# Two attention layers on 64 graphs: both plain fp32 products split in three passes, with a new order of the first slot, the steady slot and the drain

## The chip, the cores and the metric

One NeuronCore of a Trainium2 chip runs the whole program. The metric is the device time of one execution in microseconds; the kernel before takes 312.04 us (median of 3 runs, 311.88 to 312.27). Names of engines: PE is TensorE, DVE is VectorE, ACT is ScalarE, POOL is GpSimd, SP is SyncE, which here issues every DMA.

## The reference, cut to what matters

```python
def reference(x, adj, nodemask, Wqk, Wv, Wq_w, Wq_b, Wk_w, Wk_b, Wv_w, Wv_b):   # x (64,128,256), adj (64,128,128)
    # layer 0
    q, k = split(x @ Wqk); v = x @ Wv
    agg = einsum('bij,bjd->bid', adj, k * mask)
    w = mask * einsum('bid,bid->bi', q, agg) / 16
    x = layernorm(x + softmax(w, axis=1)[:, :, None] * v)
    # layer 1
    query, key, value = x @ Wq_w.T + Wq_b, x @ Wk_w.T + Wk_b, x @ Wv_w.T + Wv_b
    weight = adj * exp(einsum('bqd,bkd->bqk', query, key))
    weight = weight / sum(weight, axis=2)
    return layernorm(x + einsum('bqk,bkd->bqd', weight, value))
```

## The kernel before

The 64 graphs are taken in 32 pairs. The program on each engine is a list of slots, t = -2 to 29, and then a `drain()` written out by hand. A slot works on several pairs at once: layer 0 of pair t+2, the normalisation between the layers of pair t+1, queries, values and scores of pair t, the attention product of pair t-1, and the output of pair t-3. Slots 4 to 27 are a hardware loop unrolled four times; the others stand written out, and slots with r of -2, -1, 0 and DRAIN (29) have steps of their own. There is no scheduler: the order on each engine is the order of the code in `slot(t, r)`, and semaphores bind the engines.

Weights are folded first: layer 0's scores need only `x·(Wq Wk^T)·(adj x)`, so `aggregate` forms adj·x, `project` forms x·M0 and x·Wv together (512 columns), and `weight` on DVE multiplies and sums. `transpose_w`, a row maximum, `exp_row` on ACT, `inv_sum` and `p_row` on DVE make the softmax over the nodes, `transpose_p` turns it into a column, and `sum_x1` adds p·v to x. Statistics (`both_stats`, `neg_mean`, `var_eps`) are on DVE, the root and the shift (`rstd`, `shift`) on POOL, and the normalisation itself (`norm`) on ACT.

Most products are already split: an operand is written as hi + lo in the format F32R, and `split_half` (L748 to L750) runs hi·hi, hi·lo and lo·hi. Two products of each slot are plain fp32 matmuls: `aggregate` (L765) and `attend` (L845). One plain fp32 product shows in the trace as two matmul records, so the two graphs of a pair make four. On PE the slot is: transposes of x1, aggregate, project graph 0, attend, project graph 1, queries, transpose_w, values, scores, transpose_p. The two halves of a split are made by copies to F32R on ACT or DVE (`x1t_hi` L537, `xt_hi` L390) and by a subtraction on DVE or POOL (`x1t_lo` L539, `xt_lo` L344). POOL's slot holds five instructions: `rstd`, `shift`, `xt_lo`, `x1b` (x1 plus the value bias) and `adjm` (adj times the mask).

Of the kernel before, what the change touches and what calls it, by code (L numbers as in the profile page):

```python
# [32 lines left out]
def build(nc, x_pairs, xt_pairs, adjt_pairs, params0, params1, value_bias, out_pairs):  # L33
    ctx = ExitStack()
    with ctx:  # L35
# [348 lines left out]
        def _(act):  # L384
            def split_xt(u, r):

                act.wait_ge(xt_loaded[r % 2], transfers2(u, r))
# [4 lines left out]

# [23 lines left out]
            def drain():  # L416
# [12 lines left out]
                act.wait_ge(x1t_lo_done, b + 1)
                nc.scalar.copy(x1t[:, :, :, :], x1t_drain_ps).then_inc(x1t_copied, 1)  # L430
                act.wait_ge(val_done, a + 1)
                nc.scalar.copy(val[:, :, 0:DIM], val_ps[:, :, 0:DIM]).then_inc(val_copied, 1)
                act.wait_ge(z_done, b + 1)
                bias_z(z_b)
# [565 lines left out]
```

## Time and profile before

| | |
|---|---|
| median of 3 runs | 312.04 us |
| the profiled execution | 311.97 us |
| its span, first to last instruction | 310.1 us |
| busy: PE | 298.0 us (96%) |
| busy: DVE, ACT, POOL | 223.6 (72%), 195.8 (63%), 143.2 (46%) |
| granted TensorE clock, mean | 0.993 |

The span is the time between the first and the last instruction; the profiled execution takes 1.87 us more than that. A busy share is a mean over the whole span. Durations of single instructions overlap their neighbours on the same engine by some hundredths to tenths of a microsecond, so what an instruction costs its engine is the distance from its start to the next start, where nothing is waited for.

### The profile page before, as it was taken

To read this page: it belongs to the slowest core of one execution; us is meant where nothing else is said; L and a number is where in the kernel's file an instruction comes from. 1 tells how busy PE (TensorE), PEld (TensorE's weight loads), DVE (VectorE), ACT (ScalarE), POOL (GpSimd) and SP (SyncE) were. 2 spreads that over 40 slices of the span, in tenths; PEclk is the share of its full clock that TensorE was granted. 3 is DMA by queue.
4 is the path that set the end of the run, shared out by engine and by line. 5 is a ranking of instruction groups with operands and counts; after the bars stand their busy time and mean duration, and the time that the engine had idled before them with its cause. 6 is when DMAs were issued, how large, how long until landed. Compare 5 with 4: busy or idle time off the path is not lost. (4 is left out here: it accounts for less than half of the span.)

```text
span 310.1 us, 6526 instructions
## 1 busy us (share of the span) xinstructions
PE 298.0 (96%) x1900; PEld 269.3 (87%) x1900; DVE 223.6 (72%) x691; ACT 195.8 (63%) x453; POOL 143.2 (46%) x181
## 2 busy tenths in 40 slices
PE   8997999999999999999999999999999999999891
PEld 6876999999998999999998999999999999999780
DVE  2475778777778877777788777778877777788565
ACT  4354556676666666766666676666666766665761
POOL 2365554345555444455543345555443455542522
PEclk9999999999999999999999999999999999999997
DMA  6921224232434332234333222444423234210012
GB/s 231 327 71 35 85 88 116 52 113 83 118 119 119 119 91 80 80 105 119 119 119 111 83 73 90 118 119 119 119 85 83 81 107 119 85 53 36 34 36 101
DMA packets 19165, 31.26 MB, mean 101 GB/s; under 512 B 2128, under 2 KB 6608, under 8 KB 19152
## 3 DMA queue, kind: packets, MB, share of 16 engines
q1 hardware_dynamic: 19152, 31.11, 32.8%
q8 instruction: 6, 0.10, 0.1%
q14 instruction: 7, 0.06, 0.1%
HBM read 22.71 MB, written 8.39 MB: 100 GB/s over the span
## 5 line engine op out<-in xcount | busy, mean ns | idle before, releaser
L336 POOL TENSOR_TENSOR rstd<-var_eps,minus_half 128x4 f32<-128x4 f32 x31 | 31.5, 1018 | 138.6 <-DVE var_eps L669 124.5
L396 ACT ACTIVATE x<-x_sum,shift,rstd 128x256 f32<-128x256 f32 x62 | 34.0, 595 | 52.2 <-POOL shift L339 52.2
L748 PE MATMUL ps<-w_hi,xt_hi 128*128 128x512 f32 x128 | 61.6, 481 | 0.5 <-DVE w_lo L734 0.5
L750 PE MATMUL ps<-w_hi,xt_lo 128*128 128x512 f32 x128 | 50.4, 394 | 0.0
L749 PE MATMUL ps<-w_lo,xt_hi 128*128 128x512 f32 x128 | 50.2, 393 | 0.0
L275 POOL TENSOR_TENSOR x1b<-x,bv_all 128x512 f32<-128x512 f32 x32 | 41.5, 1297 | 4.3 <-DVE x L568 3.1
L344 POOL TENSOR_TENSOR xt_lo<-xt_raw,xt_hi 128x512 fp32r<-128x512 f32 x31 | 40.0, 1291 | 3.3 <-ACT xt_hi L390 3.3
L748 PE MATMUL ps<-wv_hi,x1t_hi 128*128 128x258 f32 x124 | 37.8, 304 | 0.0
L396 ACT ACTIVATE x<-x,shift,rstd 128x256 f32<-128x256 f32 x62 | 33.8, 595 | 3.5 <-POOL shift L287 3.5
L750 PE MATMUL ps<-wv_hi,x1t_lo 128*128 128x258 f32 x124 | 35.3, 285 | 0.0
L748 PE MATMUL ps<-x1t_hi,at_hi 128*128 128x256 f32 x124 | 35.1, 283 | 0.0
L749 PE MATMUL ps<-wv_lo,x1t_hi 128*128 128x258 f32 x124 | 35.1, 283 | 0.0
L749 PE MATMUL ps<-x1t_lo,at_hi 128*128 128x256 f32 x124 | 35.0, 282 | 0.0
L750 PE MATMUL ps<-x1t_hi,at_lo 128*128 128x256 f32 x124 | 34.8, 281 | 0.0
L409 ACT ACTIVATE z<-ps,z_bias 128x256 f32<-128x256 f32 x62 | 26.0, 470 | 11.3 <-PE ps L750 11.3
L524 DVE CUSTOM_DVE_ANT_0 agg<-ps,agg,adjt 128x256 f32<-128x256 f32 x64 | 30.9, 484 | 2.9 <-PE ps L750 0.8
L765 PE MATMUL ps<-x_raw,adjm 128*128 128x256 f32 x128 | 32.9, 380 | 0.0
L840 PE MATMUL ps<-x1t,z 128*128 128x128 f32 x240 | 31.8, 275 | 0.6 <-ACT z L409 0.6
L845 PE MATMUL ps<-val,edge 128*128 128x258 f32 x124 | 32.1, 380 | 0.0
L549 DVE SCALAR_TENSOR_TENSOR x_sum<-ps,p_col,x_raw 128x256 f32<-128x256 f32 x64 | 28.0, 479 | 3.2
L840 PEld LDWEIGHTS ps<-x1t,z 128*128 128x128 f32 x240 | 29.3, 191 | 0.8 <-ACT z L409 0.8
L748 PEld LDWEIGHTS ps<-w_hi,xt_hi 128*128 128x128 f32 x128 | 24.1, 188 | 5.7 <-issue 0.9
(121 smaller groups left out, 668.8 us busy)
## 6 DMA issues: line engine op xcount, KB each, us to landing
xt_raw<-xt_pairs SPq DMA_DIRECT2D x32, 256.0 KB, 2.7
x_raw<-x_pairs SPq DMA_DIRECT2D x32, 256.0 KB, 2.7
out_pairs<-x SPq DMA_DIRECT2D x31, 256.0 KB, 2.1
adjt<-adjt_pairs SPq DMA_DIRECT2D x32, 129.0 KB, 2.1
p<-params SPq DMA_DIRECT2D x1, 770.0 KB, 6.8
p<-params SPq DMA_DIRECT2D x1, 512.0 KB, 3.9
p<-params SPq DMA_DIRECT2D x1, 256.0 KB, 4.9
out_pairs<-x SPq DMA_DIRECT2D x2, 128.0 KB, 1.8
```

The lines of the kernel that those rows point to most:

```text
L275: nc.gpsimd.tensor_tensor(x1b[r % 2][:, :].rearrange("p (g d) -> p g d", g=2), x1[r % 2][:, :].rearrange("p (g d) -> p g d", g=2), bv_all[ ...
L336: nc.gpsimd.tensor_tensor(rstd[r % 2][:, :, :], var_eps[:, :, :], minus_half[:, :, :], ALU.pow)\
L344: nc.gpsimd.tensor_tensor(xt_lo[(r + 3) % 2][:, :, :, :].rearrange("p t g n -> p (t g n)"), xt_raw[(r + 3) % 2][:, :], xt_hi[(r + 3) % 2][ ...
L396: last = nc.scalar.activation(out[:, graph(g)], in_[:, graph(g)], ACT.Identity, bias=shift[r % 2][:, layer, g:g + 1], scale=rstd[r % 2][:, ...
L524: nc.vector.tensor_tensor_reduce(agg[:, g, :], y_ps(r)[:, g, :], agg[:, g, :], adjt[r % 4][:, PAIR_N + g:PAIR_N + g + 1], 0.0, ALU.mult, A ...
L549: nc.vector.scalar_tensor_tensor(out=x1_sum[r % 2][:, graph(g)], in0=v0_ps(r)[:, g, :], scalar=p_col[:, g:g + 1], in1=x_raw[r % 4][:, grap ...
L748: nc.tensor.matmul(out, s_hi, m_hi, start=first, stop=False)
L749: nc.tensor.matmul(out, s_hi, m_lo, start=False, stop=False)
L750: return nc.tensor.matmul(out, s_lo, m_hi, start=False, stop=last)
L765: mm = nc.tensor.matmul(agg_ps[:, g, :], adjm[r % 2][:, graph(g, NODES)], x_raw[r % 4][:, graph(g)], start=True, stop=True)
L840: mm = nc.tensor.matmul(out[:, g, :], zs[:, k, graph(g, NODES)], xs[:, k, g, :], start=(k == 0), stop=(k == HALVES - 1))
L845: return nc.tensor.matmul(out[:, g, 0:VAL_COLS], edges[:, graph(g, NODES)], vals[:, g, :], start=True, stop=True)
```

## The change

Six things change.

1. `aggregate` for pairs 4 to 31 (`SPLIT = 4`) and `attend` for pairs 0 to 28 become split products of three passes. The last three pairs keep the plain attend.
2. The halves that these need are new instructions. ACT: `edge_hi` (128x256), `adjm_hi` (128x256), `x_hi` (128x512). POOL: `low_x` makes `x_lo` (128x512), then `edge_lo` and, in `low_adjm`, `adjm_lo` (128x256 each). DVE: `val_lo` (128x512, from PSUM).
3. On PE the attention product stands behind both projections instead of between them, and the transposes of the next pair's x1 stand at the end of a slot instead of the head of the next one.
4. `exp_row` moves from SBUF to PSUM; both `weight` instructions stand together ahead of `attended`; POOL's `adjm` stands ahead of `xt_lo`.
5. First slot: `fold_biases` comes later, `transpose_w` of pair 2 stands behind the values, `bias_z` stands ahead of the norm, and POOL waits for `x1t_lo` before its first `x1b`.
6. Drain: the roles of the two last pairs' buffers are exchanged, and the attention product of pair 30 and what DVE does with it stand before the values of pair 31 and its edges.

```diff
@@ pool @@
             def slot(t, r):
+                if exists(t + 3) and r + 3 >= SPLIT:
+                    low_x(t + 3, r + 3)
+                if exists(t - 1):
+                    pool.wait_ge(edge_hi_done, t)
+                    nc.gpsimd.tensor_tensor(edge_lo[:, :], edge[:, :], edge_hi[:, :].bitcast(F32), ALU.subtract)\
+                        .then_inc(edge_lo_done, 1)
...
+                if r == -1:
+                    mask_adj(3, 3)
+                    pool.wait_ge(x1t_lo_done, 1)
...
-                if exists(t + 3) and r >= 0:
-                    mask_adj(t + 3, r + 3)
+                if exists(t + 3) and r + 3 >= SPLIT:
+                    low_adjm(t + 3, r + 3)
@@ act @@
+                if exists(t - 1):
+
+                    act.wait_ge(edge_done, t)
+                    if exists(t - 2):
+                        act.wait_ge(sum_done, t - 1)
+                    nc.scalar.copy(edge_hi[:, :], edge[:, :]).then_inc(edge_hi_done, 1)
...
+                if exists(t + 3) and r + 3 >= SPLIT:
+                    split_adjm(t + 3, r + 3)
...
+                if exists(t + 4) and r + 4 >= SPLIT:
+                    split_x(t + 4, r + 4)
@@ dve @@
+                if exists(t - 1):
+
+                    dve.wait_ge(val_copied, t)
+                    nc.vector.tensor_tensor(val_lo[:, :, 0:DIM], val_ps[:, :, 0:DIM], val_hi[:, :, 0:DIM].bitcast(F32),
+                                            ALU.subtract).then_inc(val_lo_done, 1)
...
-                    nc.vector.tensor_scalar(p_row[0:2, :], exp_row[:, :], inv_sum[:, 0:1], None, ALU.mult)\
+                    nc.vector.tensor_scalar(p_row[0:2, :], exp_row_ps(r + 2), inv_sum[:, 0:1], None, ALU.mult)\
                         .then_inc(p_row_done, 1)
@@ pe @@
+                        mm = split_product(agg_ps[:, g, :], [(adjm_hi[r % 2][:, n], adjm_lo[r % 2][:, n],
+                                                              x_hi[r % 2][:, graph(g)], x_lo[r % 2][:, graph(g)])])
...
                 if exists(t + 2):
                     project(t + 2, r + 2, 1)
+                if exists(t - 1):
+
+                    pe.wait_ge(edge_lo_done, t)
+                    pe.wait_ge(val_lo_done, t)
+                    for g in range(2):
+                        n = graph(g, NODES)
+                        mm = split_product(sum_ps[:, g, 0:VAL_COLS], [(edge_hi[:, n], edge_lo[:, n],
+                                                                       val_hi[:, g, :], val_lo[:, g, :])])
+                    mm.then_inc(sum_done, 1)
@@ drain, pe @@
                 pe.wait_ge(x1t_lo_done, b + 1)
-                pe.wait_ge(z_copied, a + 1)
                 queries(x1t_hi, x1t_lo)
-                pe.wait_ge(x2_done, DRAIN + 1)
-                scores(score_ps, z, x1t_a)
+                pe.wait_ge(edge_done, a + 1)
                 pe.wait_ge(val_copied, a + 1)
+                attend(sum_a_ps, edge_a, val_a, 0)
+                attend(sum_a_ps, edge_a, val_a, 1).then_inc(sum_done, 1)
                 pe.wait_ge(score_bias_done, a + 1)
                 values(x1t_hi, x1t_lo, 0)
```

POOL's slot in the loop before, from the copy of one slot's `xt_lo` on (a trailing number is the buffer):

```order
L344 TENSOR_TENSOR xt_lo0<-xt_raw0,xt_hi0 128x512
L275 TENSOR_TENSOR x1b0<-x1_0,bv_all 128x512
...
L267 TENSOR_TENSOR adjm0<-adjt0 128x256
...
L336 TENSOR_TENSOR rstd0<-var_eps,minus_half 128x4
L339 TENSOR_TENSOR shift0<-neg_mean,rstd0 128x4
```

The same stretch on POOL after the change:

```order
L374 TENSOR_TENSOR xt_lo1<-xt_raw1,xt_hi1 128x512
L287 TENSOR_TENSOR x1b1<-x1_1,bv_all 128x512
L342 TENSOR_TENSOR adjm_lo1<-adjm1,adjm_hi1 128x256
...
L347 TENSOR_TENSOR x_lo0<-x_raw0,x_hi0 128x512
L355 TENSOR_TENSOR edge_lo<-edge,edge_hi 128x256
...
L364 TENSOR_TENSOR rstd1<-var_eps,minus_half 128x4
L367 TENSOR_TENSOR shift1<-neg_mean,rstd1 128x4
...
L279 TENSOR_TENSOR adjm0<-adjt0 128x256
```

Between the last big instruction of one slot and `rstd` of the next there was nothing; now `x_lo` follows straight behind `adjm_lo`, and `edge_lo` behind it.

DVE in the loop before, from the column p of pair t+1 to the variance:

```order
L544 COPY p_col<-ps 128x2
L549 SCALAR_TENSOR_TENSOR x1_sum0<-ps,p_col,x_raw0 128x256 x2
L651 TENSOR_TENSOR edge<-exp_s,adjt2 128x256
L537 CAST x1t_hi<-x1t 128x512
L539 TENSOR_TENSOR x1t_lo<-x1t,x1t_hi 128x512
L530 BN_STATS stats<-x1_sum0 128x6
L668 TENSOR_SCALAR neg_mean<-stats 128x4
L669 TENSOR_SCALAR var_eps<-stats 128x4
```

and the same stretch after:

```order
L604 COPY p_col<-ps 128x2
L609 SCALAR_TENSOR_TENSOR x1_sum0<-ps,p_col,x_raw0 128x256 x2
L713 TENSOR_TENSOR edge<-exp_s,adjt2 128x256
L597 CAST x1t_hi<-x1t 128x512
L599 TENSOR_TENSOR x1t_lo<-x1t,x1t_hi 128x512
L720 TENSOR_TENSOR val_lo<-ps,val_hi 128x2x256
L590 BN_STATS stats<-x1_sum0 128x6
L735 TENSOR_SCALAR neg_mean<-stats 128x4
L736 TENSOR_SCALAR var_eps<-stats 128x4
```

`val_lo` is new and stands ahead of the statistics; the others keep their places.

## Rows read from the trace of the kernel before

**Rows 1.** Windows: stretch, length, busy us PE PEld DVE ACT POOL, clock, DMA, GB/s

```profile
47.69:280.42 232.73, 232.73 (x1511) 212.46 (x1510) 176.06 (x547) 157.04 (x364) 111.64 (x130) 1.00 0.34 100
```

**Rows 2.** Timeline of PE, one slot (start us, us, what)

```profile
155.63 1.03 PE L765 MATMUL ps<-x_raw,adjm 128*128 128x256 f32 x4
...
156.73 0.39 PE L749 MATMUL ps<-w_lo,xt_hi 128*128 128x512 f32 x1
...
157.88 1.03 PE L845 MATMUL ps<-val,edge 128*128 128x258 f32 x4
...
160.15 0.29 PE L748 MATMUL ps<-x1t_hi,at_hi 128*128 128x256 f32 x1
...
161.58 0.27 PE L791 MATMUL ps<-ident,w_col 128*2 128x128 f32 x1
```

**Rows 3.** Timeline of DVE, same slot

```profile
156.46 0.41 DVE L651 TENSOR_TENSOR edge<-exp_s,adjt 128x256 f32<-128x256 f32 x1
156.79 0.42 DVE L537 CAST x1t_hi<-x1t 128x512 fp32r<-128x512 f32 x1
157.24 0.69 DVE L539 TENSOR_TENSOR x1t_lo<-x1t,x1t_hi 128x512 fp32r<-128x512 f32 x1
157.85 0.70 DVE L530 BATCH_NORM_STATS2 stats<-x_sum 128x6 f32<-128x512 f32 x1
158.58 0.17 DVE L668 TENSOR_SCALAR neg_mean<-stats 128x4 f32<-128x4 f32 x1
```

**Rows 4.** Timeline of POOL, same slot

```profile
158.91 1.02 POOL L336 TENSOR_TENSOR rstd<-var_eps,minus_half 128x4 f32<-128x4 f32 x1 [4.48 <-DVE var_eps L669]
160.00 0.20 POOL L339 TENSOR_TENSOR shift<-neg_mean,rstd 128x4 f32<-128x4 f32 x1
160.15 1.29 POOL L344 TENSOR_TENSOR xt_lo<-xt_raw,xt_hi 128x512 fp32r<-128x512 f32 x1
161.41 1.31 POOL L275 TENSOR_TENSOR x1b<-x,bv_all 128x512 f32<-128x512 f32 x1
162.65 0.63 POOL L267 TENSOR_TENSOR adjm<-adjt 128x256 f32<-128x256 f32 x1
```

**Rows 5.** Timeline of ACT, same slot

```profile
160.23 1.10 ACT L396 ACTIVATE x<-x_sum,shift,rstd 128x256 f32<-128x256 f32 x2 [1.44 <-POOL shift L339]
161.78 0.84 ACT L409 ACTIVATE z<-ps,z_bias 128x256 f32<-128x256 f32 x2 [0.45 <-PE ps L750]
```

**Rows 6.** Timelines of POOL and of DVE, where the two meet

```profile
7.08 1.17 DVE L734 TENSOR_TENSOR w_lo<-p,w_hi 128x256 fp32r<-128x256 f32 x2
...
7.14 0.83 POOL L267 TENSOR_TENSOR adjm<-adjt 128x256 f32<-128x256 f32 x1 [5.50 <-DMA adjt<-adjt_pairs]
...
20.73 1.31 POOL L275 TENSOR_TENSOR x1b<-x,bv_all 128x512 f32<-128x512 f32 x1
...
20.90 1.43 DVE L537 CAST x1t_hi<-x1t 128x512 fp32r<-128x512 f32 x1
```

**Rows 7.** Timelines of PE and POOL, slots 0 and 1

```profile
26.07 0.27 PE L791 MATMUL ps<-ident,w_col 128*2 128x128 f32 x1 [1.29 <-DVE w_col L524]
...
28.41 1.16 PE L840 MATMUL ps<-x1t,z 128*128 128x128 f32 x8 [0.62 <-ACT z L409]
...
33.61 1.02 POOL L336 TENSOR_TENSOR rstd<-var_eps,minus_half 128x4 f32<-128x4 f32 x1 [4.06 <-DVE var_eps L669]
```

**Rows 8.** Timelines of POOL, PE and DVE, slot 29 and drain

```profile
284.23 1.02 POOL L336 TENSOR_TENSOR rstd<-var_eps,minus_half 128x4 f32<-128x4 f32 x1 [4.57 <-DVE var_eps L669]
...
288.91 0.30 PE L797 MATMUL ps<-ident,p_row 128*128 128x128 f32 x1
...
289.73 0.22 DVE L717 TENSOR_SCALAR score_bias<-ps,s_bias 128x2 f32<-128x2 f32 x1 [0.96 <-ACT val L503]
...
301.60 0.42 DVE L555 TENSOR_TENSOR edge_b<-exp_s,adjt 128x256 f32<-128x256 f32 x1 [0.74 <-ACT exp_s L403]
...
304.03 0.16 DVE L563 RECIPROCAL den_inv<-ps 128x2 f32<-128x2 f32 x1
```

More of the change, by code:

```diff
@@ L73, in build @@
         adjm = [sb(f"adjm{i}", [128, PAIR_N]) for i in range(2)]
+        x_hi = [sb(f"x_hi{i}", [128, PAIR_X], F32R) for i in range(2)]
+        x_lo = [sb(f"x_lo{i}", [128, PAIR_X], F32R) for i in range(2)]
+        adjm_hi = [sb(f"adjm_hi{i}", [128, PAIR_N], F32R) for i in range(2)]
+        adjm_lo = [sb(f"adjm_lo{i}", [128, PAIR_N], F32R) for i in range(2)]
         agg = sb("agg", [128, 2, DIM])
@@ L92, in build @@
         edge = sb("edge", [128, PAIR_N])
+        edge_hi = sb("edge_hi", [128, PAIR_N], F32R)
+        edge_lo = sb("edge_lo", [128, PAIR_N], F32R)
+        val_hi = sb("val_hi", [128, 2, VAL_COLS], F32R)
+        val_lo = sb("val_lo", [128, 2, VAL_COLS], F32R)
         den_inv = sb("den_inv", [128, 2])
@@ L326, in drain, with low_adjm, low_x @@
                 root(DRAIN, 0)
-            def slot(t, r):
+            def low_adjm(u, r):
+                pool.wait_ge(adjm_hi_done, u + 1 - SPLIT)
+                nc.gpsimd.tensor_tensor(adjm_lo[r % 2][:, :], adjm[r % 2][:, :],
+                                        adjm_hi[r % 2][:, :].bitcast(F32), ALU.subtract).then_inc(adjm_lo_done, 1)
+            def low_x(u, r):
+                pool.wait_ge(x_hi_done, u + 1 - SPLIT)
+                nc.gpsimd.tensor_tensor(x_lo[r % 2][:, :], x_raw[r % 4][:, :],
+                                        x_hi[r % 2][:, :].bitcast(F32), ALU.subtract).then_inc(x_lo_done, 1)
+            def slot(t, r):
+                if exists(t + 3) and r + 3 >= SPLIT:
[4 more added lines that the diff above has]
+                        .then_inc(edge_lo_done, 1)
                 if exists(t + 1) or exists(t - 2):
@@ L391, in split_xt, with split_x, split_adjm @@
                                xt_raw[r % 2][:, :]).then_inc(xt_hi_done, 1)
+            def split_x(u, r):
+                act.wait_ge(x_loaded[r % 4], transfers4(u, r))
+                act.wait_ge(agg_done, u - 1)
+                nc.scalar.copy(x_hi[r % 2][:, :], x_raw[r % 4][:, :]).then_inc(x_hi_done, 1)
+            def split_adjm(u, r):
+                act.wait_ge(adjm_done, u + 1)
+                act.wait_ge(agg_done, u - 1)
+                nc.scalar.copy(adjm_hi[r % 2][:, :], adjm[r % 2][:, :]).then_inc(adjm_hi_done, 1)
             def norm(out, in_, layer, r, done):
@@ L425, in drain @@
                 act.wait_ge(z_done, a + 1)
-                bias_z(z)
+                bias_z(z_a)
+                act.wait_ge(val_done, a + 1)
+                nc.scalar.copy(val_a[:, :, 0:DIM], val_ps[:, :, 0:DIM]).then_inc(val_copied, 1)
                 normed_out(DRAIN - 1, n + 1)
[L429 to L434, printed above, removed]
                 act.wait_ge(score_done, a + 1)
@@ L489, in slot @@
                     act.wait_ge(row_max_done, t + 3)
-                    nc.scalar.activation(exp_row[:, :], w_row_ps(r + 2), ACT.Exp, bias=neg_max[:, 0:1],
+                    nc.scalar.activation(exp_row_ps(r + 2), w_row_ps(r + 2), ACT.Exp, bias=neg_max[:, 0:1],
                                          accum_out=exp_sum[:, 0:1]).then_inc(row_exp_done, 1)
+                if exists(t + 3) and r + 3 >= SPLIT:
+                    split_adjm(t + 3, r + 3)
                 if r == DRAIN:
@@ L615, in drain @@
                 variance(1)
-                weigh_edges(a, edge)
-                bias_scores(b)
-                weigh_edges(b, edge_b)
                 dve.wait_ge(sum_done, a + 1)
-                attended(a, sum_ps)
+                attended(a, sum_a_ps)
                 dve.wait_ge(x2_done, a + 1)
@@ L957, in _ @@
             fold_scores(1).then_inc(at_done, 1)
-            fold_biases()
+            aggregate(1, 1)
             transpose_p(0, 0)
-            aggregate(1, 1)
             project(1, 1, 0)
             project(1, 1, 1)
+            fold_biases()
+            transpose_w(1, 1)
             aggregate(2, 2)
-            transpose_w(1, 1)
+            transpose_next(-1, -1)
             slots(pe, slot, 0)
```

142 lines of the change are left out of this document (83 added, 59 removed).

## The prediction

> **What bounds the kernel now.** I read the clock first: the granted TensorE clock is 1.00 in the steady stretch [rows 1], the level of 2.4 GHz, so the clock is not the matter. Then the busy time by stretch. From 47.69 to 280.42 us, 26 slots by the transposes of p, PE is busy for 232.73 of 232.73 us [rows 1]; that is 8.951 us a slot, and PE sets it. DVE has 176.06, ACT 157.04 and POOL 111.64 us of work in it, 6.77, 6.04 and 4.29 us a slot. Last I read the timelines of one slot: on POOL `rstd` waited 4.48 us for the variance [rows 4], ACT's norm 1.44 us for the shift and `z` 0.45 us for PE [rows 5]. The others run after PE with slack. A slot can also be counted from `rstd` to `rstd`: 33.61 in slot 1 [rows 7] and 284.23 in slot 29 [rows 8], 250.62 us for 28 slots, 8.951 again. I count in these below. The question is whether PE still sets the slot once DVE, ACT and POOL carry the work of making the halves.
>
> **The change, part by part.**
>
> PE's saving. The aggregate takes from 155.63 to 156.73, less one 512-column pass (156.73 to 157.88 is five passes of 0.23), so 0.87. The attend takes from 157.88 to 160.15, less six passes of 0.23, so 0.89. Split, each becomes six passes of 256 or 258 columns; twelve such passes take 160.15 to 161.58, 0.119 each [rows 2], so 0.72. The saving is 0.15 + 0.17 = 0.32 a slot: if PE stays the bound, a slot takes 8.63.
>
> ACT's additions. `edge_hi` and `adjm_hi` are 256 columns, `x_hi` is 512. I bound them by `z`, two instructions of 256 columns in 0.84 us: 4 x 0.42 = 1.68 us a slot at most, and by the slope alone, without what an instruction costs at its start, some 1.0. ACT had waits of 1.44 and 0.45 in the slot [rows 5]. I take 1.2 and put it off the path, since the shift comes later anyway (next part); uncovered it would be worth some tenths a slot.
>
> POOL's additions. `x_lo` is as large as `xt_lo`, 1.29 us; `edge_lo` and `adjm_lo` are as large as `adjm`, 0.63 [rows 4]. That is 2.55 us on 4.29, 6.8 of 8.9. By the sum it fits. By its place it may not. From `rstd` on POOL now runs without a gap: `rstd` 1.09 (158.91 to 160.00), `shift` 0.15, `adjm` 0.58 (0.63 less 0.05, the overlap with the next), `xt_lo` 1.26 (160.15 to 161.41), `x1b` 1.24 (to 162.65), `adjm_lo` 0.58, and then `x_lo` for 1.29. The sum is 6.19 us after the start of `rstd` [rows 4]. Before, POOL was idle in that last part, and there DVE makes `edge`, `x1t_hi` and `x1t_lo` [rows 3].
>
> POOL and DVE in one another's way. Two places of the trace show what happens when they meet [rows 6]. A cast of 512 columns SBUF to SBUF, 0.42 us in the slot [rows 3], took 1.43 from 20.90, under POOL's `x1b` of 20.73 to 22.04; it ended at 22.33, 0.29 after POOL. The second of two subtractions with both operands in SBUF ended at 8.25, 0.28 after POOL's `adjm` (7.97), and `adjm` itself took 0.83 instead of 0.63, from behind the first of them [rows 6]. So such an instruction on DVE does not end before POOL's current one has, and vice versa. `edge` and `x1t_lo` have two operands in SBUF and `x1t_hi` is that cast. `val_lo` reads PSUM for one operand; I take it as free of this.
>
> The Trainium skill, SBUF — State Buffer, section "Who interferes with whom", says that a DVE instruction with two SBUF inputs or in a two-port mode and a GpSimd instruction exclude each other, and that the loser waits for the other's whole length. The rows agree on who is blocked, but the blocked one ended 0.28 us after the other where a full one takes 0.41; by the page's words each block would cost 0.13 more and the sum below would be 27 x 0.13 = 3.5 us higher.
>
> Now the path. On ACT `exp_s` stands behind `x_hi`, and `edge` needs `exp_s`; POOL's `x_lo` needs only `x_hi`. So `edge` always comes when `x_lo` has begun or POOL is still in front of it. Then the loop from one `rstd` to the next is: 6.19 to the end of `x_lo`; 0.28 to the end of `edge`; `x1t_hi` begins 0.08 before that (156.46 + 0.41 against 156.79) and takes 0.45 to the next start, `x1t_lo` 0.61, `val_lo` 0.61 (as `x1t_lo`), the statistics 0.73, and `neg_mean` and the variance 0.33 to the start of `rstd` (158.58 to 158.91) [rows 3, 4]. Sum: 6.19 + 0.28 - 0.08 + 0.45 + 0.61 + 0.61 + 0.73 + 0.33 = 9.12 us. That is longer than PE's 8.63 and also than the 8.951 of before. I take 9.15, since `x_lo` also waits for `x_hi`, which comes about when POOL is free. `val_lo` is the one term without a row of its own: its bounds are 0.33 (as `edge` to the next start, for 256 columns) and 0.73 (the statistics of 512), so 8.84 to 9.24.
>
> Slots. `x_lo` is made in slots 1 to 28, so 27 distances from slot 1 to slot 28 take 9.15 and the last one PE's 8.65: 255.7 us against 250.62, **+5.1**.
>
> Start. In slot 0 PE waited 1.29 us for the weights and 0.62 for `z` [rows 7]; `transpose_w` now stands behind the values and `bias_z` ahead of the norm, and both waits should go, -1.91. In slot 1 `val_lo` (0.61) and the first block of `edge` (0.33, an estimate: 9.12 less the 8.79 that the loop has without it, rival a) are already in the way: **-0.97** in all.
>
> Drain. PE is no longer late in slot 29, so `z` follows the norm without its wait of 0.45 [rows 5]: -0.45. `p_col` stood behind `score_bias`, which waited 0.96 us for the copy of the values, until 289.73 + 0.13, where the transpose of p (288.91) had ended by 289.2 [rows 8]; now `p_col` is ahead: -0.6. The attend of pair 30 comes before the values of pair 31 and costs PE 0.89 there, but the values of pair 30 need not be finished between, and scores and queries only change places; I count 0. At the end `edge_b` was ready at 302.02; with an attend of 0.88 and 0.2 of latency the sum could be read at 303.1, but DVE took it up at 304.03, busy with pair 30 [rows 8]. Pair 30 is now done earlier: -0.8 (bounds 0 and -0.9). Drain: **-1.85**.
>
> Other edits. `exp_row` in PSUM, the order of `weight`, `neg_max` and `stats2`, and `adjm` ahead of `xt_lo` I cost at nothing: DVE has 2.2 us free a slot, less 0.6 for `val_lo`. The transposes of x1 at a slot's end instead of its head are the same work in the same place. The attend behind both projections is free as long as PE has slack; `edge_lo` and `val_lo` must be there about 3.5 us after the aggregate begins.
>
> **The sum.** The profiled execution took 311.97 us, 1.87 more than its span of 310.1, and stands 0.07 below the median of 312.04. 311.97 - 0.97 + 5.1 - 1.85 = 314.25: I forecast 314.2 us. A measurement of this kernel can tell about 0.2% (0.6 us) from no change.
>
> **Rivals.**
>
> (a) `edge` slips in ahead of `x_lo`, and only the cast is held. Then the loop is 6.19 + 0.29 + 0.03 + 0.61 + 0.61 + 0.73 + 0.33 = 8.79. For it: POOL may come late to `x_lo`, since `x_hi` is the last in ACT's slot. Against: `exp_s` is behind `x_hi`. Slots 27 x 8.79 + 8.65 = 246.0, -4.6; start -1.3, drain -1.85: 304.2 us.
>
> (b) PE stays the bound; nothing of POOL is on the path. 28 x 0.32 = -9.0, start -1.9, drain -1.4 (the wait of `z` stays): 299.7 us. For it: by busy time nothing else is full. Against: the loop above has 0.5 us too much.
>
> (c) `edge_lo` gets in between `x1t_hi` and `x1t_lo`. `edge_hi` takes about 0.37 from the end of `edge`, and with 0.08 for the two hand-overs `edge_lo` is ready 0.45 after it; `x1t_lo` begins 0.37 after it. If POOL wins, `x1t_lo` ends at 0.45 + 0.63 + 0.56 instead of 1.06 and every slot is 0.58 longer: 27 x 0.58 = +15.7, 329.9 us. This decides at 0.08 us. The same page of the Trainium skill says that issue order decides who blocks; by that `x1t_lo` wins, and the time stays at the forecast.
>
> (d) The gains at both ends don't come, because other waits stand behind those removed: +2.8, 317.0 us.
>
> **Chances.** Forecast 0.52, with its own range 311 to 318 (the bounds of `val_lo` and of the block); (a) 0.20, (b) 0.11, (c) 0.10, (d) 0.07. Of the forecast's 0.52 I put 0.38 above 312.7, 0.08 within 0.6 us of 312.04, and 0.06 below. Slower: 0.38 + 0.10 + 0.07 = 0.55; same 0.08; faster 0.06 + 0.20 + 0.11 = 0.37. The range is 303.5 to 321: it takes in (a) and (d) and leaves out (b) and (c).
>
> **What the new profile would show.** PE idle some 0.5 us a slot, most of it ahead of the aggregate, for `adjm_lo` of POOL; `edge` at 1 us or more instead of 0.41, ending 0.28 after `x_lo`; `rstd` to `rstd` 9.15; the matmul records of aggregate and attend at 0.12 spacing; `x1t_lo` at its 0.69. I would be wrong if `edge` still takes 0.41 (rival a or b), if PE is busy throughout (b), or if `x1t_lo` takes more than 1 us (c). At the ends: no wait of PE above 0.5 us in slot 0, and the last `den_inv` within 1.2 us of the end of the last edges.

## The result, and the profile after

The changed kernel takes 316.99 us (median of 4 runs, 316.78 to 317.20), the kernel before 311.96 in the same comparison (4 runs, 311.78 to 312.27). The ratio is 1.016 with a 95% interval of 1.0143 to 1.0178: 1.6% slower, 5.0 us, where I had forecast 2.2. The profiled execution took 316.78 us, with a span of 315.0 against 310.1.

The page of the kernel after, busy time by engine (us, share of the span, instructions):

```profile
PE 300.7 (95%) x2014; PEld 269.4 (86%) x2014; DVE 252.1 (80%) x720; ACT 218.3 (69%) x538; POOL 228.5 (73%) x269
```

The stretch that answers to [rows 1], 26 slots from `rstd` to `rstd`, in the same columns:

```profile
41.03:281.81 240.78, 236.56 (x1614) 212.65 (x1614) 203.77 (x573) 177.81 (x442) 190.21 (x208) 1.00 0.31 97
```

The granted clock is again 1.00, so it is not the matter. PE now sits idle for 4.22 us, which it did not before. POOL went from 4.29 to 7.3 us of work a slot (190.21 / 26), and with 1.9 us left no sum of busy times names it as the bound.

The span splits at `rstd` of slot 1 and of slot 29, as in the prediction:

| part | before | after | difference | forecast |
|---|---|---|---|---|
| start, to `rstd` of slot 1 | 33.61 | 31.84 | -1.77 | -0.97 |
| slots 1 to 29 | 250.62 | 258.60 | +7.98 | +5.1 |
| `rstd` of slot 29 to the end | 25.87 | 24.56 | -1.31 | -1.85 |
| span | 310.1 | 315.0 | +4.9 | +2.3 |

Timeline of POOL after, one slot, what answers to [rows 4] (start us, us, engine, line, what, the idle time before it and its releaser):

```profile
142.97 1.02 POOL L364 TENSOR_TENSOR rstd<-var_eps,minus_half 128x4 f32<-128x4 f32 x1 [1.06 <-DVE var_eps L736]
144.07 0.20 POOL L367 TENSOR_TENSOR shift<-neg_mean,rstd 128x4 f32<-128x4 f32 x1
144.22 0.61 POOL L279 TENSOR_TENSOR adjm<-adjt 128x256 f32<-128x256 f32 x1
144.79 1.29 POOL L374 TENSOR_TENSOR xt_lo<-xt_raw,xt_hi 128x512 fp32r<-128x512 f32 x1
146.04 1.27 POOL L287 TENSOR_TENSOR x1b<-x,bv_all 128x512 f32<-128x512 f32 x1
147.27 0.73 POOL L342 TENSOR_TENSOR adjm_lo<-adjm,adjm_hi 128x256 fp32r<-128x256 f32 x1
147.96 1.28 POOL L347 TENSOR_TENSOR x_lo<-x_raw,x_hi 128x512 fp32r<-128x512 f32 x1
150.04 1.15 POOL L355 TENSOR_TENSOR edge_lo<-edge,edge_hi 128x256 fp32r<-128x256 f32 x1 [0.80 <-ACT edge_hi L517]
152.25 1.02 POOL L364 TENSOR_TENSOR rstd<-var_eps,minus_half 128x4 f32<-128x4 f32 x1 [1.05 <-DVE var_eps L736]
```

Timeline of DVE after, same slot, what answers to [rows 3]:

```profile
148.55 0.98 DVE L713 TENSOR_TENSOR edge<-exp_s,adjt 128x256 f32<-128x256 f32 x1
149.45 0.41 DVE L597 CAST x1t_hi<-x1t 128x512 fp32r<-128x512 f32 x1
149.90 0.69 DVE L599 TENSOR_TENSOR x1t_lo<-x1t,x1t_hi 128x512 fp32r<-128x512 f32 x1
150.50 0.69 DVE L720 TENSOR_TENSOR val_lo<-ps,val_hi 128x512 fp32r<-128x512 f32 x1
151.10 0.71 DVE L590 BATCH_NORM_STATS2 stats<-x_sum 128x6 f32<-128x512 f32 x1
151.85 0.17 DVE L735 TENSOR_SCALAR neg_mean<-stats 128x4 f32<-128x4 f32 x1
```

Read the two together. From `rstd` at 142.97 POOL has no gap until `x_lo` ends at 149.24. `edge`, 0.41 us long before, was begun under `x_lo` and ended at 149.53, 0.29 after it. From there DVE has no gap to the variance, and that releases the next `rstd`. This closed loop of two engines, each of which is idle at some other point of the slot, takes 9.28 us here.

The same tiles over the whole program (duration in ns: shortest, median, longest):

```profile
L713 DVE TENSOR_TENSOR edge<-exp_s,adjt x29: 415/981/1007, 28.7 to 287.4; 128x256 f32<-128x256 f32 x29
L355 POOL TENSOR_TENSOR edge_lo<-edge,edge_hi x29: 737/1143/1150, 29.7 to 288.9; 128x256 fp32r<-128x256 f32 x29
L342 POOL TENSOR_TENSOR adjm_lo<-adjm,adjm_hi x28: 716/738/753, 36.1 to 286.1; 128x256 fp32r<-128x256 f32 x28
```

`edge` is held in 28 of its 29 cases; only the last, at 0.415, is not. `edge_lo` is held too, by `x1t_lo` ahead of it, but POOL has 1.05 us to spare there. (In e4 below, where `x1t_lo` reads PSUM, `edge_lo` takes 0.74.)

PE in the same slot, the transposes of x and the first passes of the aggregate, which answer to the head of [rows 2]:

```profile
147.31 0.63 PE L898 MATMUL ps<-ident,x 128*128 128x128 f32 x4
148.06 0.38 PE L813 MATMUL ps<-x_hi,adjm_hi 128*128 128x256 f32 x1
148.28 0.28 PE L814 MATMUL ps<-x_lo,adjm_hi 128*128 128x256 f32 x1
148.40 0.28 PE L815 MATMUL ps<-x_hi,adjm_lo 128*128 128x256 f32 x1
```

The waits of PE in the stretch (us in total, times, longest us):

```profile
PEld ps L813 <- POOL adjm_lo L342: 7.6, 20, 0.4
```

The aggregate waits for `adjm_lo`, which ends at 148.00. The busy figure shows little of it: the record of the transposes runs to 147.94, and only the 0.12 us behind that counts as idle.

### The profile page after: what moved, and what is told of

It is laid out like the page before. It is cut to its first block and busy times, and to the rows that moved or that the text cites. A ratio compares the mean times of both kernels' runs of the same rounds, so it can differ in the third digit from the quotient of the medians.

```text
span 315.0 us, 7064 instructions
## 1 busy us (share of the span) xinstructions
PE 300.7 (95%) x2014; PEld 269.4 (86%) x2014; DVE 252.1 (80%) x720; ACT 218.3 (69%) x538; POOL 228.5 (73%) x269
## 5 line engine op out<-in xcount | busy, mean ns | idle before, releaser
L813 PE MATMUL ps<-w_hi,xt_hi 128*128 128x512 f32 x128 | 50.7, 396 | 0.7 <-DVE w_lo L799 0.7
L355 POOL TENSOR_TENSOR edge_lo<-edge,edge_hi 128x256 fp32r<-128x256 f32 x29 | 32.0, 1102 | 25.3 <-ACT edge_hi L517 25.3
L347 POOL TENSOR_TENSOR x_lo<-x_raw,x_hi 128x512 fp32r<-128x512 f32 x28 | 36.2, 1292 | 0.1
L916 PE MATMUL ps<-x1t,z 128*128 128x128 f32 x248 | 35.6, 286 | 0.0
L916 PEld LDWEIGHTS ps<-x1t,z 128*128 128x128 f32 x248 | 30.0, 191 | 4.2 <-ACT z L456 2.4
L584 DVE CUSTOM_DVE_ANT_0 agg<-ps,agg,adjt 128x256 f32<-128x256 f32 x64 | 28.6, 482 | 1.0 <-PE ps L815 1.0
L815 PEld LDWEIGHTS ps<-w_hi,xt_lo 128*128 128x128 f32 x128 | 24.0, 188 | 5.3
```

The costliest lines, as they stand in the source:

```text
L347: nc.gpsimd.tensor_tensor(x_lo[r % 2][:, :], x_raw[r % 4][:, :], x_hi[r % 2][:, :].bitcast(F32), ALU.subtract).then_inc(x_lo_done, 1)
L355: nc.gpsimd.tensor_tensor(edge_lo[:, :], edge[:, :], edge_hi[:, :].bitcast(F32), ALU.subtract)\
L584: nc.vector.tensor_tensor_reduce(agg[:, g, :], y_ps(r)[:, g, :], agg[:, g, :], adjt[r % 4][:, PAIR_N + g:PAIR_N + g + 1], 0.0, ALU.mult, A ...
L813: nc.tensor.matmul(out, s_hi, m_hi, start=first, stop=False)
L815: return nc.tensor.matmul(out, s_lo, m_hi, start=False, stop=last)
L916: mm = nc.tensor.matmul(out[:, g, :], zs[:, k, graph(g, NODES)], xs[:, k, g, :], start=(k == 0), stop=(k == HALVES - 1))
```

## The experiments

The slot is (`rstd` of slot 29 less `rstd` of slot 1) / 28, from the profile of each. Each ratio is to the runs of before in the same comparison, whose medians lie between 311.96 and 312.25 us.

| kernel | us (range) | ratio to before, 95% | slot, us | `edge`, median us |
|---|---|---|---|---|
| before | 311.96 (311.78 to 312.27) | 1 | 8.951 | 0.415 |
| after | 316.99 (316.78 to 317.20) | 1.016 (1.0143 to 1.0178) | 9.236 | 0.981 |
| e1_neither | 307.11 (306.65 to 307.57) | 0.9828 (0.9812 to 0.9845) | 8.887 | 0.416 |
| e2_attend_only | 304.01 (303.86 to 304.14) | 0.9734 (0.9717 to 0.9750) | 8.780 | 0.415 |
| e3_aggregate_only | 304.80 (304.78 to 305.08) | 0.9762 (0.9746 to 0.9779) | 8.796 | 0.703 |
| e4_psum_both | 310.97 (310.82 to 311.38) | 0.9959 (0.9944 to 0.9973) | 9.011 | 0.415 |
| e5_xlo_behind | 319.00 (318.92 to 319.21) | 1.0220 (1.0203 to 1.0237) | 9.301 | 0.415 |
| e6_psum_edge | 308.35 (308.20 to 308.46) | 0.9876 (0.9859 to 0.9892) | 8.931 | 0.415 |
| e7_early_adjm | 316.01 (315.99 to 316.60) | 1.0123 (1.0106 to 1.0140) | 9.211 | 0.54 |
| e8_two_pool_extras | 307.21 (306.93 to 307.39) | 0.9840 (0.9823 to 0.9856) | 8.883 | 0.614 |
| e9_adjm_lo_ahead | 317.67 (317.50 to 317.90) | 1.0172 (1.0155 to 1.0189) | 9.254 | 0.68 |
| e10_psum_and_ahead | 310.14 (309.90 to 310.45) | 0.9929 (0.9912 to 0.9946) | 8.994 | 0.415 |
| e11_two_pool_extras_full | 316.73 (316.44 to 316.90) | 1.0148 (1.0131 to 1.0165) | 9.223 | 0.969 |

**Which part costs.** e1_neither keeps the new drain, first slot and order and leaves both products plain.

```diff
-SPLIT = 4
+SPLIT = PAIRS
...
-                    nc.gpsimd.tensor_tensor(edge_lo[:, :], edge[:, :], edge_hi[:, :].bitcast(F32), ALU.subtract)\
-                        .then_inc(edge_lo_done, 1)
...
-                    nc.scalar.copy(edge_hi[:, :], edge[:, :]).then_inc(edge_hi_done, 1)
...
+                    attend(sum_ps, edge, val, 0)
+                    attend(sum_ps, edge, val, 1).then_inc(sum_done, 1)
```

> The new start, order of the slot and drain, with both products left as plain fp32 matmuls. Theory 1 (POOL's x_lo holds DVE's edge back, which makes a slot 9.26 us): nothing is left that holds, so a slot is PE's 8.95 again and only the ends count. First rstd of slot 1 about 1.9 us earlier than before, tail after slot 29 about 1.4 us shorter: about 309 us. Theory 2 (the new order of the slot, attend behind both projections and transposes at the end, costs PE something): a slot above 8.95, total 312 or more.

e2_attend_only splits the attention product alone; the aggregate stays plain.

```diff
-SPLIT = 4
+SPLIT = PAIRS
...
-                if exists(t + 3) and r + 3 >= SPLIT:
+                if exists(t + 3) and r >= 1:
                     mask_adj(t + 3, r + 3)
```

> Only the attention product is split; the aggregate is plain, so x_hi, adjm_hi, x_lo and adjm_lo are gone, val_lo, edge_hi and edge_lo stay. Theory 1: edge takes 0.41 us, PE is the bound with 8.95 - 0.17 = 8.78 a slot; 309 - 28 x 0.17 = about 304 us. Theory 3 (val_lo ahead of the statistics and the two hand-overs edge, edge_hi, edge_lo make the slot long, whatever x_lo does): the slot stays at 9.0 or more and the time above 312.

e3_aggregate_only splits the aggregate alone: `SPLIT` stays 4, and the edits of e1_neither on the edges and the values stand, so that `edge_hi`, `edge_lo` and `val_lo` are not made.

> Only the aggregate is split; val_lo, edge_hi and edge_lo are gone, x_lo and adjm_lo stay. Theory 1: edge is still held by x_lo (about 0.9 us instead of 0.41), but the loop from rstd to rstd lacks val_lo: 9.26 - 0.60 = 8.66, below PE's 8.95 - 0.15 = 8.80, so PE is the bound and the time about 304.5 us. Theory 4 (PE waits for adjm_lo, the last of POOL's slot, and that alone sets the slot): PE idle ahead of the aggregate, slot 9.0 or more, 312 or more.

e1 came out 1.9 us below the 309 expected, since its slot is 8.887 and not 8.95; e2 and e3 came out as theory 1 said. Each part by itself gains over e1's 307.11: 3.1 us and 2.3 us. Together they lose 9.9. So neither product and neither end of the program is slow; the two sets of halves can't be had in one slot. In e3 `x_lo` still holds `edge` (0.70), but without `val_lo` DVE's part of the loop is 0.60 shorter, 9.26 - 0.60 = 8.66, less than the slot of 8.80, and PE is busy for 237.36 of 237.36 us from 40.63 to 277.99. In e2 POOL is done with `x1b` before `edge` comes:

```profile
L713 DVE TENSOR_TENSOR edge<-exp_s,adjt x29: 411/415/417, 28.7 to 274.6; 128x256 f32<-128x256 f32 x29
```

and PE is busy for 228.60 of 228.60 us from 41.58 to 270.18: there PE is the bound again.

**Is it the block?** In e6_psum_edge ACT writes `exp_s` to PSUM, so that `edge` reads one operand from SBUF and one from PSUM. POOL's work is unchanged.

```diff
+        exp_ps = ps[:, 3:5, 384:512]
...
-                    exp_scores(score_ps)
+                    exp_scores(score_ps, exp_ps)
...
-                    nc.vector.tensor_tensor(edge[:, :], exp_s[:, :], adjt[(r - 1) % 4][:, 0:PAIR_N], ALU.mult)\
+                    nc.vector.tensor_tensor(pairs(edge), exp_ps, pairs(adjt[(r - 1) % 4]), ALU.mult)\
```

> Only exp_s in PSUM, so only edge is freed of POOL; x1t_hi and x1t_lo stay SBUF to SBUF. Theory 1a (POOL's next instruction goes first when it is ready before DVE's): edge and edge_hi are done while x_lo still runs, edge_lo follows straight behind x_lo, and x1t_hi waits for both: x1t_hi above 1.5 us, a slot 6.27 + 0.71 + 0.29 + 0.03 + 0.61 + 0.60 + 0.73 + 0.32 = about 9.55, 325 us. Theory 1b (DVE's, which has waited longer, goes first): x1t_hi ends 0.29 after x_lo, a slot about 8.95, 309 us.

e4_psum_both does the same, and lets `x1t_hi` and `x1t_lo` read their source from PSUM too.

```diff
-                nc.vector.tensor_copy(x1t_hi[:, :, :, :], x1t[:, :, :, :]).then_inc(x1t_hi_done, 1)
+                nc.vector.tensor_copy(x1t_hi[:, :, :, :], x1t_ps).then_inc(x1t_hi_done, 1)
...
-                nc.vector.tensor_tensor(x1t_lo[:, :, :, :], x1t[:, :, :, :], x1t_hi[:, :, :, :].bitcast(F32),
+                nc.vector.tensor_tensor(x1t_lo[:, :, :, :], x1t_ps, x1t_hi[:, :, :, :].bitcast(F32),
```

> The whole change, no order touched: exp_s of the slots lies in PSUM, and x1t_hi and x1t_lo read the transposes in PSUM instead of their copy, so that edge and the two x1t instructions have one SBUF operand and no fast mode. Theory 1: edge is 0.41 to 0.45 us although x_lo runs beside it, x1t_hi is 0.69 instead of 0.41; the slot falls to 8.85 (PE with some waits for adjm_lo), about 306 us. Theory 3 (the loop is long by its work): x1t_hi adds 0.27 us a slot, 317 + 7 = 324 us.

Timelines of POOL and DVE of e6:

```profile
180.13 1.30 POOL L351 TENSOR_TENSOR x_lo<-x_raw,x_hi 128x512 fp32r<-128x512 f32 x1
...
184.10 1.02 POOL L368 TENSOR_TENSOR rstd<-var_eps,minus_half 128x4 f32<-128x4 f32 x1 [1.05 <-DVE var_eps L740]
...
180.77 0.41 DVE L717 TENSOR_TENSOR edge<-ps,adjt 128x256 f32<-128x256 f32 x1
181.10 0.62 DVE L601 CAST x1t_hi<-x1t 128x512 fp32r<-128x512 f32 x1
181.75 0.69 DVE L603 TENSOR_TENSOR x1t_lo<-x1t,x1t_hi 128x512 fp32r<-128x512 f32 x1
```

`edge` now runs in its full 0.41 us while `x_lo` runs. 8.6 us of the time come back (316.99 to 308.35) with every half still made. This is theory 1b, at 309 us; 1a, at 325, is out. What is left is the same loop one instruction further: the cast `x1t_hi`, 0.42 long where nothing holds it, is held in three slots of four (0.53 to 0.65) and ends here at 181.72, 0.29 after `x_lo` (181.43); then 0.03 to `x1t_lo`, and 2.35 us from there to `rstd`. With 6.29 from `rstd` (175.14) to the end of `x_lo` that is 8.96, what this slot takes. This is rival (a)'s loop, which I had put at 8.79. In e4 the loop is cut at the cast as well, but the cast from PSUM is longer by itself, and the time is 310.97, not the 306 expected (timeline of DVE of e4):

```profile
153.71 0.22 DVE L639 TENSOR_SCALAR score_bias<-ps,s_bias 128x2 f32<-128x2 f32 x1 [0.25 <-ACT val_hi L565]
...
155.33 0.68 DVE L601 CAST x1t_hi<-ps 128x512 fp32r<-128x512 f32 x1
156.05 0.69 DVE L603 TENSOR_TENSOR x1t_lo<-ps,x1t_hi 128x512 fp32r<-128x512 f32 x1
```

Nothing is held in this slot, which takes 8.89 from the `rstd` at 149.42. It runs through a third engine: the shift releases ACT's norm (150.75), ACT works without a gap to the end of `val_hi` (153.67), that releases `score_bias`, and DVE has only hand-overs of about 0.1 us and less from there to the variance. In one slot of four `p_col` also waits 0.26 us for PE, and the slot takes 9.22; the mean is 9.01. So with the block out of the way ACT's part of the slot comes next, with the new `adjm_hi` in it (0.29 to the next start).

The Trainium skill, SBUF — State Buffer, section "Who interferes with whom", says that a DVE instruction with at most one SBUF input, outside the 2-port modes, does not contend with GpSimd. The trace agrees for `edge` (0.41 beside `x_lo` in e6, 0.98 with both operands in SBUF), and for `val_lo`, of which the prediction took it: in e4 `val_lo` and `edge_lo` run side by side in all 29 slots, at 0.68 and 0.74 to 0.75.

**The block without anything that waits.** e8_two_pool_extras and e11_two_pool_extras_full are e2_attend_only, the fast one, with two subtractions added on POOL where the change has `adjm_lo` and `x_lo`. Nobody reads their results or waits for them, and they wait only for the loads that they read. In e8 both operands are the same tile.

```diff
+                    nc.gpsimd.tensor_tensor(x_lo[v % 2][:, :], x_raw[v % 4][:, :], x_raw[v % 4][:, :], ALU.subtract)
...
+                    nc.gpsimd.tensor_tensor(adjm_lo[(r + 3) % 2][:, :], a, a, ALU.subtract)
```

> The kernel of e2 (only the attention product split, 304.0 us) with two subtractions added on POOL, of the size and in the places of adjm_lo and x_lo; they read x_raw, write tiles that nobody reads, and nobody waits for them. ACT and PE have no more to do than in e2. Theory 1 (POOL holds DVE's edge back): POOL is busy until 6.27 us after rstd again, edge is held to about 1 us, a slot is 6.27 + 2.93 = 9.20 and the time 304 + 27 x 0.42 = about 315.5 us. Theory 4 (the whole change is slow since PE waits for the halves, and ACT is fuller): 304 to 305.5 us, POOL's idle time takes both.

They turned out shorter than the originals (timelines of POOL and DVE of e8):

```profile
160.65 0.63 POOL L399 TENSOR_TENSOR adjm_lo<-x_raw 128x256 fp32r<-128x256 f32 x1
161.22 1.06 POOL L354 TENSOR_TENSOR x_lo<-x_raw 128x512 fp32r<-128x512 f32 x1
...
161.97 0.60 DVE L716 TENSOR_TENSOR edge<-exp_s,adjt 128x256 f32<-128x256 f32 x1
```

0.63 and 1.06 where `adjm_lo` and `x_lo` take 0.73 and 1.28, and the time rose by 3.2 us only, not by the 11.5 expected. `x_lo` ends 0.36 us earlier in the loop (5.91 after `rstd`, against 6.27), and with 0.28 and 2.70 from there to the next `rstd` the loop is 8.89, for a measured slot of 8.883: the loop gives the small rise as well. e11 repeats it with two different tiles.

```diff
+                    nc.gpsimd.tensor_tensor(x_lo[v % 2][:, :], x_raw[v % 4][:, :], p0[:, 0:PAIR_X], ALU.subtract)
...
+                    nc.gpsimd.tensor_tensor(adjm_lo[(r + 3) % 2][:, :], x_raw[(r + 3) % 4][:, 0:PAIR_N],
+                                            p0[:, 0:PAIR_N], ALU.subtract)
```

> As e8, with the two idle instructions made as long as adjm_lo and x_lo really are: each now subtracts the weights from x_raw, two different tiles, where e8 subtracted x_raw from itself and took 0.63 and 1.05 us instead of 0.74 and 1.29. Nobody reads or awaits the results. The loop of theory 1 is the end of the second one after rstd plus 2.93: 6.27 + 2.93 = 9.20 a slot against 8.78 in e2, 304 + 27 x 0.42 = about 315.5 us. If the length of a slot comes from ACT's and PE's share of the change, it stays at e8's 307.2 or below.

```profile
156.74 0.73 POOL L399 TENSOR_TENSOR adjm_lo<-x_raw,p 128x256 fp32r<-128x256 f32 x1
157.42 1.29 POOL L355 TENSOR_TENSOR x_lo<-x_raw,p 128x512 fp32r<-128x512 f32 x1
...
161.65 1.02 POOL L367 TENSOR_TENSOR rstd<-var_eps,minus_half 128x4 f32<-128x4 f32 x1 [0.98 <-DVE var_eps L740]
...
158.03 0.97 DVE L717 TENSOR_TENSOR edge<-exp_s,adjt 128x256 f32<-128x256 f32 x1
```

`edge` again ends 0.29 after POOL's instruction (159.00 and 158.71). The time is 316.73 us: two instructions without a reader took 12.7 us from a kernel of 304.0, and brought it within 0.3 of the whole change. ACT's casts `adjm_hi` and `x_hi`, PE's passes of the split aggregate and its wait for `adjm_lo` are absent here, so they are not the cause. `edge_hi`, `edge_lo` and `val_lo` are there, as they are in e2, which takes 304.0 us with them.

**Attempts to move POOL's work away.** e5_xlo_behind puts `x_lo` behind `edge_lo`.

```diff
-                if exists(t + 3) and r + 3 >= SPLIT:
-                    low_x(t + 3, r + 3)
                 if exists(t - 1):
                     pool.wait_ge(edge_hi_done, t)
...
+                if exists(t + 3) and r + 3 >= SPLIT:
+                    low_x(t + 3, r + 3)
```

> The whole change with one thing moved: on POOL x_lo stands behind edge_lo instead of ahead of it. Theory 1 (x_lo holds edge back): edge takes 0.41 us; but edge_lo is still held by x1t_lo and x_lo must now end before rstd. From rstd: edge ends at about 6.0, x1t_lo at 7.0, edge_lo at 7.7, x_lo at 9.0, so a slot is about 9.0 and rstd no longer waits for the variance: 317 - 27 x 0.25 = about 310 us. Theory 5 (POOL's sum of work plus what it shares with DVE sets the slot, wherever x_lo stands): no change, 316 to 318 us.

It frees `edge` (0.415) and is slower all the same, since the block moved (timelines of POOL and DVE of e5):

```profile
161.28 1.29 POOL L347 TENSOR_TENSOR x_lo<-x_raw,x_hi 128x512 fp32r<-128x512 f32 x1
162.75 1.02 POOL L364 TENSOR_TENSOR rstd<-var_eps,minus_half 128x4 f32<-128x4 f32 x1 [0.18 <-DVE var_eps L736]
...
161.82 0.77 DVE L735 TENSOR_SCALAR neg_mean<-stats 128x4 f32<-128x4 f32 x1
```

`neg_mean`, 16 bytes a partition and 0.17 us long elsewhere, was held for 0.77, to 162.59, where `x_lo` ended at 162.57; and `rstd` stood behind it. `x_lo` ends 9.06 us after `rstd` (153.51), as I had expected; the block of the statistics, which I had not, makes 9.24 of it, and the time is 319.0 us instead of 310.

e7_early_adjm makes `adjm` ahead of `rstd`, in POOL's idle time, and `adjm_lo` right behind the shift.

```diff
+                if exists(t + 3) and r + 3 >= SPLIT:
+                    mask_adj(t + 3, r + 3)
                 if exists(t + 1) or exists(t - 2):
...
-                    mask_adj(t + 3, r + 3)
+                    low_adjm(t + 3, r + 3)
```

> The whole change with adj times mask made before rstd, in POOL's idle time, its high part on ACT before the norm of x1, in ACT's idle time, and adjm_lo right behind shift. Theory 1: x_lo ends 5.72 us after rstd instead of 6.27, the loop is 5.72 + 2.93 = 8.65, edge is still held (about 1 us) but PE is the bound at 8.69 (8.89 of the kernel with neither split, less 0.11 and 0.09 as the two single splits show); 317 - 27 x 0.57 = about 302 us. Theory 5 (POOL's sum sets the slot): the same instructions in another order change little, 315 to 318 us.

It gained 1.0 us of the 316.99, far less than I expected. `x_lo` does end 0.44 us earlier after `rstd` (5.84), but `neg_mean` to `rstd` is 0.79 instead of 0.38 (means of the slots), which takes 0.42 of it back. The load of `adjt` comes too late for `adjm`, which then holds `neg_mean` or the variance in most slots, and `rstd` stands behind it in any case (timelines of POOL and DVE of e7):

```profile
160.91 0.64 POOL L279 TENSOR_TENSOR adjm<-adjt 128x256 f32<-128x256 f32 x1 [0.65 <-DMA adjt<-adjt_pairs]
...
160.99 0.59 DVE L736 TENSOR_SCALAR var_eps<-stats 128x4 f32<-128x4 f32 x1
```

e9_adjm_lo_ahead takes away PE's wait for `adjm_lo`: `adjm_hi` stands ahead of `z` on ACT, and `adjm_lo` ahead of `x1b` on POOL. e10_psum_and_ahead is e9 with the PSUM operand of e6.

```diff
+                if exists(t + 3) and r + 3 >= SPLIT:
+                    low_adjm(t + 3, r + 3)
                 if exists(t + 1):
...
+                if exists(t + 3) and r + 3 >= SPLIT:
+                    split_adjm(t + 3, r + 3)
                 if exists(t) and r != 0:
```

> The whole change with adjm_hi before z on ACT and adjm_lo before x1b on POOL, so that PE gets adjm_lo about 1.2 us earlier; x_lo still ends 6.27 us after rstd. Theory 1: PE's wait ahead of the aggregate goes and turns up elsewhere in its slot, the slot stays 9.25, 316.5 to 317.5 us. Theory 4 (the wait for adjm_lo sets the slot): PE's 0.5 us of idle time goes, about 304 us.

> The whole change with exp_s in PSUM (e6) and adjm_lo ahead as in e9. With edge no longer held, e6 had a slot of 8.93 and PE waited for adjm_lo; if that wait is what is late next, the slot falls to PE's 8.69 to 8.75 and the time to 302 to 303.5 us. If something else of the loop is late (x1t_hi behind x_lo, the norm behind POOL), it stays at 308.

Both missed a gain. e9 is no faster than after (ratios of 1.0172 and 1.016, with intervals that overlap), and e10 is 1.8 us slower than e6. In e9 PE now waits for `z`, which ACT makes later (waits of e9, 100 to 250 us):

```profile
PEld ps L916 <- ACT z L456: 8.4, 17, 0.6
```

The order within POOL's chain does not change its length: `x_lo` ends 6.28 us after `rstd` as before, and `edge` 0.28 after it. With this loop as the bound, removing a wait of PE had nothing to give.

In e10 it is another loop. There `edge` ends with `x_lo`, and the cast is not held (timeline of DVE of e10):

```profile
154.09 0.16 DVE L608 COPY p_col<-ps 128x2 f32<-128x2 f32 x1 [0.32 <-PE ps L877]
...
155.47 0.42 DVE L601 CAST x1t_hi<-x1t 128x512 fp32r<-128x512 f32 x1
```

`adjm_hi` stands in front of `z` on ACT and puts it off by 0.30 us (151.59 to 151.89); PE's scores follow `z` (152.76), the transpose of p follows the scores (153.76), and `p_col` waits for that. From `p_col` to `rstd` at 158.20 DVE goes on as in the other kernels. So e10 pays on ACT and PE for the wait that it removed.

## Why the prediction was right on the sign and too small on the size

**The mechanism held.** I said that `edge` would end 0.28 after `x_lo`, on a loop of POOL and DVE longer than PE's slot. It ends 0.27 to 0.30 after it, and e11 and e6 show the block as the cause by adding it alone and by taking it away.

**The step that failed is the size of the loop**, and within it two terms. The sum was 9.12, the value taken 9.15; the 27 distances from 31.84 to 281.81 are 9.258 each, 27 x 0.108 = 2.9 us more than forecast. That is the +7.98 against +5.1. The two terms below make 0.16 a slot, of which 0.03 was in the value taken and 0.02 came back in the others.

- `adjm_lo` was 0.58, from the row of `adjm` [rows 4]. It takes 0.69 to the next start (147.27 to 147.96), and its own duration is 0.738, not 0.63. `adjm` reads one column broadcast as its second operand, `adjm_lo` reads two whole tiles. The element count was the same, the operand was not, and e8 and e11 show that alone: 0.63 with the same tile twice, 0.73 with two tiles. +0.11 a slot.
- `neg_mean` to `rstd` was 0.33, from the one slot of [rows 3, 4]. In this trace it is 0.33 or 0.32 in one slot of four and 0.40 in the three others (151.85 to 152.25, and 161.12 to 161.44 a slot later); the trace of before has both as well (113.85 to 114.25, and 158.58 to 158.91), and 0.47 or 0.48 in one slot of four, a mean of 0.39 in the loop. The rows that I read were of the short kind: +0.05 on the mean.
- The other terms held within 0.02: `rstd` 1.10, `adjm` 0.57, `xt_lo` 1.25, `x1b` 1.23, `x_lo` 1.28, `x1t_hi` 0.45, `x1t_lo` 0.60, `val_lo` 0.60, the statistics 0.75. `val_lo`, which had no row, came within its bounds and at the value taken.

**Start: -1.77 against -0.97.** Timelines of PE and POOL after, slots 0 and 1, what answers to [rows 7], with `rstd` of slot 0:

```profile
25.44 0.27 PE L867 MATMUL ps<-ident,w_col 128*2 128x128 f32 x1
25.55 1.05 PE L916 MATMUL ps<-x1t,z 128*128 128x128 f32 x8
...
27.28 0.30 PE L873 MATMUL ps<-ident,p_row 128*128 128x128 f32 x1 [0.24 <-DVE p_row L778]
...
23.80 1.03 POOL L364 TENSOR_TENSOR rstd<-var_eps,minus_half 128x4 f32<-128x4 f32 x1 [0.77 <-DVE var_eps L736]
...
31.84 1.02 POOL L364 TENSOR_TENSOR rstd<-var_eps,minus_half 128x4 f32<-128x4 f32 x1 [0.98 <-DVE var_eps L736]
```

Both waits are gone, 1.91 us, and one of 0.24 has come. The distances between the first three `rstd` tell the parts:

| | first `rstd` | to that of slot 0 | to that of slot 1 | there |
|---|---|---|---|---|
| before | 17.10 | 8.10 | 8.41 | 33.61 |
| e1 | 17.33 | 7.17 | 7.33 | 31.83 |
| after | 16.63 | 7.17 | 8.04 | 31.84 |

In e1, without `val_lo` and without a block, the new order saves 2.01 us over the two distances (forecast 1.91). After takes 0.71 more in the second: that is `val_lo`, 0.60, and the first block of `edge`, 0.53 instead of 0.41, where I had charged 0.94. What makes the start look better than forecast is mostly the first 16.63 us, 0.47 less than before. No edit explains that: e1 and e9 have the same code up to there and reach it at 17.33 and 17.14, each in the one profile that was taken. So -1.77 is -0.47, -2.01 and +0.71, and the 0.47 is luck as far as the runs tell.

**Drain: -1.31 against -1.85.** Timelines of POOL, PE and DVE, what answers to [rows 8]:

```profile
290.44 1.02 POOL L364 TENSOR_TENSOR rstd<-var_eps,minus_half 128x4 f32<-128x4 f32 x1 [0.82 <-DVE var_eps L736]
...
294.86 0.27 PE L873 MATMUL ps<-ident,p_row 128*128 128x128 f32 x1
...
295.24 0.16 DVE L604 COPY p_col<-ps 128x2 f32<-128x2 f32 x1 [0.72 <-PE ps L873]
...
307.19 0.46 DVE L615 TENSOR_TENSOR edge<-exp_s,adjt 128x256 f32<-128x256 f32 x1 [0.74 <-ACT exp_s L450]
308.88 0.17 DVE L623 RECIPROCAL den_inv<-ps 128x2 f32<-128x2 f32 x1 [1.23 <-PE ps L921]
```

From `rstd` to the transpose of p 4.42 instead of 4.68 (-0.26, forecast -0.45). From there to `p_col` 0.38 instead of 0.95, if `p_col` began behind the 0.13 of `score_bias` at 289.86 (-0.57, forecast -0.6). From the end of the last edges to `den_inv` 1.23 instead of 2.01 (-0.78, forecast -0.8). Against these, the middle of the drain, which I counted as 0, is 0.25 longer (12.41 from `p_col` to the end of the last edges instead of 12.16), and 0.05 lies behind `den_inv`.

**The rivals.** (a): in after `edge` does not slip ahead; e6 takes its place and gives 8.93 a slot and 308.35 us, where I had 8.79 and 304.2, short by the same two terms. (b): PE is not the bound, and it would not have given 299.7. The saving that I gave PE was too large: against e1 the split attend saves 0.107 a slot and the split aggregate 0.091, not 0.17 and 0.15; e1's own order saves 0.064 (8.951 to 8.887), which I had at nothing. If these savings add up, PE's slot would be 8.69 (an estimate from three profiles). Why the passes save less than their spacing says is open; the passes stand 0.12 apart as forecast (148.28 to 148.40). (c): `x1t_lo` went first, at 0.69, and `edge_lo` behind it took 1.14. (d) named the time, 317.0, with the wrong reason: the gains at the ends came, 3.08 us where 2.82 were forecast (2.61 without the 0.47 of the first stretch).

**PE's idle time.** I said 0.5 us a slot; it is 4.22 / 26 = 0.16. The wait is there: from the transposes of x to the aggregate 0.75 us (147.31 to 148.06) against 0.43 (155.20 to 155.63 in the trace of before), 0.32 more, of which the modelled ends of the records cover all but 0.12. Measured by the slot, 9.26 less PE's 8.69 (the estimate above), PE loses some 0.57 us, near what I had said; the busy time does not show it.

The better kernel is e2_attend_only: new ends and order, attention product split, aggregate plain. It takes 304.0 us, 2.7% less than before and 13.0 us less than the change as made.

## What to carry to other kernels

Before moving work to an engine with free time, draw the closed loop that it joins, and look at what the neighbour does in that time: POOL was 46% busy, and two more instructions of 0.73 and 1.29 us on it, which nobody waits for, cost 12.7 us. Size an added instruction by a row with the same kinds of operands, not only the same element count, and read a recurring hand-over in several slots, since an error of 0.1 us is multiplied by their number. When two edits gain one by one and lose together, look for a resource that both lean on, and try an operand in another memory before trying another place.
